# One of the opening input transfers is issued by ScalarE on its own queue instead of by SyncE

## The reference

```python
xn = _gn(x)                          # per sample and group of 16 channels, over H and W
Wc = conv_w[:, :, 0, 4]
def step(prev, x_i):
    y = einsum('oc,nch->noh', Wc, prev) + conv_b[None, :, None]
    y = where(y >= 0, y, prelu_a * y)
    cur = y + x_i
    return (cur, cur)
# forward scan over the 48 columns, then the backward scan over the forward result
out = x + moveaxis(concatenate([bwd_rest, fl[-1:]]), 0, 3)
```

## Time and profile before

| | us |
|---|---|
| median of three runs | 376.42 |
| lowest and highest | 376.38, 376.47 |
| the profiled execution | 376.38 |
| its span in the trace | 374.6 |
| PE busy | 351.7 |
| DVE busy | 286.0 |
| ACT busy | 230.0 |
| POOL busy | 17.3 |

### The profile page before, as it was taken

The page is one execution under the profiler, slowest core; times in us unless marked ns, Lnnn a source line. Parts: engine busy times, 40 slices in busy tenths (PEclk is TensorE's granted clock), DMA queues, the critical chain, the costliest instruction groups (busy, mean ns, idle before and its releaser), DMA issues.

```text
span 374.6 us, 10099 instructions
## 1 busy us (share of the span) xinstructions
PE 351.7 (94%) x3100; PEld 350.6 (94%) x3100; DVE 286.0 (76%) x925; ACT 230.0 (61%) x810; POOL 17.3 (5%) x30
## 2 busy tenths in 40 slices
PE   0279999999999999999999999999999999999996
PEld 0179999999999999999999999999999999999996
DVE  2688899788887887665666878778778787787786
ACT  2886656656556566565565665655656657566564
POOL 2078000000000000000000000000000000000000
PEclk9999999999999999999999999999999999999999
DMA  8998000000000000000000121211212212122122
GB/s 308 429 412 308 2 0 1 0 0 0 1 0 0 1 0 0 0 0 0 0 0 0 59 84 56 84 66 73 84 56 84 82 58 84 61 79 84 56 112 84
DMA packets 10088, 26.30 MB, mean 70 GB/s; under 512 B 1248, under 2 KB 1504, under 8 KB 9440
## 3 DMA queue, kind: packets, MB, share of 16 engines
q1 hardware_dynamic: 10080, 26.22, 18.1%
HBM read 13.63 MB, written 12.58 MB: 70 GB/s over the span
## 4 chain that ended last, share of the span: by engine, by line
PE 91%; DMA 6%; SPq 1%; DVE 1%; ACT 1%; issue 0%; ACTq 0%
PE psum L352 88%; DMA xin<-in_x 6%; PE psum L312 1%; SPq L234 1%; PE psum L302 1%; DVE state L535 0%; DVE state L530 0%; ACT state L382 0%; ACT state L376 0%; PE psum L277 0%; PE psum L273 0%; PE psum L266 0%; ACT above L445 0%; PE psum L295 0%; PE psum L289 0%
## 5 line engine op out<-in xcount | busy, mean ns | idle before, releaser
L352 PE MATMUL psum<-state,w_t 128*128 (+1 forms) x2976 | 332.6, 275 | 0.0
L352 PEld LDWEIGHTS psum<-state,w_t 128*128 128x128 f32 x2976 | 332.5, 192 | 0.0
L445 ACT ACTIVATE above<-psum,params 128x128 f32<-128x128 f32 x376 | 139.7, 372 | 129.6 <-PE psum L352 128.7
L530 DVE TENSOR_TENSOR state<-above,state 128x128 f32 (+1 forms) x376 | 108.4, 288 | 66.1 <-ACT above L445 56.4
L447 ACT ACTIVATE below<-psum,negative 128x128 f32<-128x128 f32 x376 | 139.9, 372 | 0.0
L535 DVE SCALAR_TENSOR_TENSOR state<-below,negative,state 128x128 f32 (+1 forms) x376 | 123.4, 349 | 6.7
L582 DVE TENSOR_TENSOR state<-state,xin (+1 forms) x45 | 30.8, 684 | 0.0
L475 DVE TENSOR_SCALAR state<-xin,mean,rstd 128x320 f32<-128x320 f32 (+2 forms) x72 | 27.9, 435 | 0.0
L457 DVE BATCH_NORM_STATS2 bstat<-xin 128x6 f32<-128x512 f32 x32 | 20.0, 672 | 8.7 <-DMA xin<-in_x 8.7
L266 PE MATMUL psum<-chan,centre 128*128 128x64 f32 (+1 forms) x8 | 2.1, 361 | 18.7 <-DVE chan L471 18.7
L266 PEld LDWEIGHTS psum<-chan,centre 128*128 128x128 f32 x8 | 1.6, 251 | 19.0 <-issue 15.5
(11 more groups left out here) (38 smaller groups left out, 24.6 us busy)
## 6 DMA issues: line engine op xcount, KB each, us to landing
out_y<-state SPq DMA_DIRECT2D x47, 256.0 KB, 2.0
xin<-in_x SPq DMA_DIRECT2D x5, 1536.0 KB, 12.8
xin<-in_x SPq DMA_DIRECT2D x3, 768.0 KB, 21.8
xin<-in_x SPq DMA_DIRECT2D x7, 256.0 KB, 18.1
w_t<-in_w SPq DMA_DIRECT2D x4, 256.0 KB, 10.6
xin<-in_x SPq DMA_DIRECT2D x1, 512.0 KB, 24.1
out_y<-state SPq DMA_DIRECT2D x1, 192.0 KB, 1.9
out_y<-state SPq DMA_DIRECT2D x1, 64.0 KB, 1.6
```

Of the source, the lines that this page charges most:

```text
L352: mm = nc.tensor.matmul(psum[:, 4 * par + o, 0:COLS], w_t[:, k, o * P:(o + 1) * P], xs[k], start=k == 0, stop=k == 3)
L445: nc.scalar.activation(above[:, par, o, :], z, ACT.Relu, bias=params[:, o:o + 1], scale=1.0).then_inc(above_done, 1)
L530: nc.vector.tensor_tensor(sts[o], above[:, par, o, :], sts[o], ALU.add).then_inc(part_done, 1)
```

## The change

The transfer of blocks 2 and 3 leaves SyncE's program and becomes ScalarE's first instruction. Its source, its destination and its semaphore are the same; it goes to ScalarE's own DMA queue. SyncE issues all others in the same order as before, so that its second transfer is now that of blocks 4 and 5.

```diff
--- before.py
+++ after.py
@@ -23,6 +23,8 @@
 PAIRS = {0: 1, 2: 3, 4: 5, 6: 7, 8: 9}
+
+FROM_ACT = 2
 
@@ -227,7 +229,7 @@
         @block.sync
         def _(sp):
-            for b in (b for b in range(NBLK) if b not in PAIRS.values()):
+            for b in (b for b in range(NBLK) if b not in PAIRS.values() and b != FROM_ACT):
                 n1 = (PAIRS[b] if b in PAIRS else b) % N + 1
@@ -361,6 +363,9 @@
         @block.scalar
         def _(act):
+            n0, n1 = FROM_ACT % N, PAIRS[FROM_ACT] % N + 1
+            act.dma_start(xin[:, FROM_ACT // N, n0:n1, :, :], x[FROM_ACT // N, :, n0:n1, :, :]).then_inc(
+                x_loaded[FROM_ACT][0], 16)
             act.wait_ge(counts_set, 6)
```

## The result

The changed kernel takes 380.03 us (median of six runs, 379.93 to 380.18), the kernel before 376.45 us beside it (376.38 to 376.53, six runs). The ratio is 1.0096, 95% interval 1.0086 to 1.0105: slower by 3.58 us. The forecast was 379.8. The profiled execution took 380.03 us at a span of 378.0, against 376.38 and 374.6 before.

The account below looks back on a forecast made before the run. The first transfer's landing at 7.2 us was taken to set, through ScalarE and PE's queue, the start of a fixed-length scan. 376.38 us plus 3.4 us of later landing gave 379.8 us; range 377.0 to 380.4.

Parts of the forecast that it names:

- The scan is a block of fixed length.: Scan's products on PE: no idle time in front of them, so a change in loads moves only their start.
- Two issues moved, worth nothing.: Programs of SyncE (one issue less, 0.42 us) and ScalarE (one more, 0.38 to 0.42 us while idle): no time gained or lost.
- The engines take turns packet by packet.: Opening loads: two queues share by packet, so the first transfer lands 3.4 us later; chance 0.68.
- a lead of one packet: Opening loads: first transfer one packet ahead on each engine finishes one turn earlier, 3.2 us late instead of 3.65.
- The first rival: Opening loads: first transfer keeps its landing near 7.2 us, time 376.4 us; chance 0.15.
- The lag passes to PE in full.: Opening, ScalarE to PE: batch 1's records come 3.4 us later, PE's deviations at 24.9 us, and PE's queue follows.
- "PE, with no idle time to close, sets the end, and both the keep-up products' pace and their number stay.": End of the opening: PE's queue passes the delay on, so the scan starts 3.4 us later (35.35 becomes 38.75).
- The sum.: Whole kernel: 376.38 us of the profiled execution plus 3.4 us gives 379.8 us.
- "These two arrive at the end only some 2.3 us late": End of the opening: ScalarE and VectorE close up their waits and come only some 2.3 us late.
- the low end of 378.5: Whole kernel: both low ends, 3.2 - 1.1 = 2.1 us, with VectorE's 2.3 as the bound if PE's pace came at fixed time.
- block 2 is third in ScalarE's line, not fourth: ScalarE's opening: block 2 was taken as fourth in line, so its earlier landing gains nothing.
- Faster opening.: Loads' start, third rival: second queue fills the engines 0.5 us sooner, first transfer served first, 375.9 us; chance 0.04.

Follow-up runs that it names:

- experiment 9: Changed kernel with ScalarE's issue of blocks 2 and 3 moved behind its wait for the constants, to 1.7 us: 377.41 us, ratio 1.0029.
- the four kernels of this kind: Kernels with two pairs on two queues: the changed one (380.03 us), experiment 1, experiment 7 and the first kernel of experiment 10.
- experiment 2: Changed kernel with only block 3 (768 KB) on ScalarE's queue; SyncE sends blocks 0 and 1, then 2: 377.98 us, ratio 1.0042.
- experiment 3: Changed kernel with ScalarE sending blocks 2 and 3 as two transfers of 768 KB (6 KB packets): 378.15 us, ratio 1.0045.
- experiment 4: Changed kernel with SyncE sending block 0 alone (6 KB packets), then block 1; ScalarE still sends blocks 2 and 3: 377.84 us, ratio 1.0033.
- experiment 6: Kernel before with only the parameters (2.5 KB) moved to the head of ScalarE's program: 376.95 us, ratio 1.0012.
- experiment 1: Changed kernel with queues exchanged: ScalarE issues blocks 0 and 1, SyncE all others: 380.11 us, ratio 1.0098.
- experiment 7: Changed kernel with ScalarE issuing blocks 8 and 9 first instead of 2 and 3: 379.77 us, ratio 1.0090.
- experiment 5: Blocks 2 and 3 on ScalarE's queue as in experiment 3, but cut into eight transfers of 12 columns (1.5 KB packets): 391.44 us, ratio 1.0401.
- experiment 8: Changed kernel with ScalarE waiting for blocks 0 and 1 to land before issuing blocks 2 and 3: 382.68 us, ratio 1.0165.
- first kernel of experiment 10: Changed kernel with the first group of keep-up products cut from 12 in the trace to 4: 379.65 us, ratio 1.0084.
- experiment 11: Kernel before, all on SyncE's queue, with block 0 sent alone ahead of block 1: 376.66 us, ratio 1.0006.

## Why the prediction was right

The direction, the size and the mechanism held; 380.03 us lies in the range of 377.0 to 380.4 and 0.2 us from the forecast. What carries the lag to the end was not what the prediction named, and that the total is so close is partly luck. By its steps:

- **The scan is a block of fixed length.** Shown: 332.6 us of products in both, and VectorE's first state update of the scan goes from 37.90 to 41.30, its last from 372.15 to 375.55, both by 3.40.
- **Two issues moved, worth nothing.** SyncE's and ScalarE's part were right (0.40 us at 0.79, ScalarE idle until 10.95). But experiment 9 shows that the moment of the issue is not free to choose: 0.9 us later is worth 2.6 us (380.03 to 377.41).
- **The engines take turns packet by packet.** The term was 3.4 us (3.2 with a lead of one packet, 3.65 without) and measured 3.74: no lead, the upper end and a little over, 3.50 to 4.05 in the four kernels of this kind. Equal counts in the changed kernel and nearly equal ones in experiments 2, 3, 4 and 6 show the turns; experiments 2, 3 and 4 exclude sharing by bytes. The Trainium skill, page DMA: Bandwidth & Descriptors, section Queues, rings and completion order, says that an engine goes round robin between rows at packet granularity. The trace agrees if a packet is what the profile counts (17 against 17 in a microsecond). If each of these were one of the typical 9 to 17 descriptors that the page gives for a packet, the first transfer's 8 on an engine could have gone in one turn and kept their landing, and it lost 3.74 us.
- **The first rival (landing kept, 376.4 us)** fell in the changed kernel, but it describes experiment 9 in part: there the first queue does finish most of what was queued first. The same page of the Trainium skill says, in its section Issuing engines are not separate DMA queues, that transfers interleave whichever engine starts them, and that several issuing engines only save issue time. The bandwidth bears that out (418 GB/s with two queues). But the interleaving changed what lands first, and that cost 1% of the time; "only saves", taken alone, would have missed it.
- **The lag passes to PE in full.** 3.73 us at the deviations of batch 1, shown.
- **"PE, with no idle time to close, sets the end, and both the keep-up products' pace and their number stay."** Both halves were wrong. The 20 products took 2.96 us, not 3.52, so that PE's side came only 3.2 us late. And POOL sets the end, which the prediction never followed: it starts its last stretch 3.73 us late and has 0.32 us to give, which is 3.40. PE's faster pace gave the scan nothing: in experiment 1 the 20 products took 3.48 us, and VectorE's first state update is 0.33 us less late than the first use of block 0 (3.72 against 4.05), here 0.34 (3.40 against 3.74).
- **The sum.** 3.4 us was the middle between two landings, and the span grew by 3.40 because the landing came 0.34 us later than taken and POOL had 0.32 us of idle time. These two cancel by luck. The rest of the 3.65 us between the profiled executions lies outside the span; some 0.1 of it goes with the second queue (experiment 6), and the prediction had no term for it.
- **"These two arrive at the end only some 2.3 us late"** was wrong. VectorE's last channel record goes from 34.29 to 37.32 us, 3.0 late. I let both engines close their waits for transfers and forgot that ScalarE waits for PE's variances behind the keep-up products (0.91 us at 29.39) and VectorE for ScalarE (0.90 at 30.95). It made no difference to the forecast, as PE was taken to set the end; but the low end of 378.5 rests on it and was too low. (In the same place block 2 is third in ScalarE's line, not fourth, which changes nothing.)
- **Faster opening.** 253 GB/s between 1.75 and 3.50 us with two queues against 281 with one: the second queue doesn't fill the engines sooner.

Open: why the pace of the keep-up products differs. The same 20 took 3.52, 2.96, 3.48, 3.31, 2.77 and 2.53 us (the kernel before, the changed one, experiments 1, 7, 3, 9), at a granted clock of 1.00, or 0.999. It doesn't set the scan's start in those with blocks on the second queue: in the changed kernel and experiments 1 to 5 and 7 to 9, the multiplication that releases the scan stands 10.12 to 10.16 us behind the start of POOL's power of batch 1 (29.73 to 39.87 in the changed one), whatever the pace, and in all but experiment 1 VectorE waits for POOL there. Only the first kernel of experiment 10, where PE's side holds the scan, is apart (10.74 us).

## What to carry to other kernels

When the DMA engines are full, a second queue doesn't add transfers but reorders them: what was to land first now shares with what was to land second, packet against packet, so give everything that the first work waits for the engines to itself, and look at packet sizes, since the queue with the smaller packets loses. Before moving a transfer, list what each landing is waited for by, and how long behind it there is no slack; here one landing at 7.2 us had next to none, and the one moved ahead some 1.7 us (an estimate: landed near 10.87, first used by ScalarE at 12.56). A gain at a point where two limits meet is worth nothing (experiment 11), a loss there is paid nearly in full. And follow every engine that works without a pause up to the end, also one that is busy for 5% of the span: here POOL's line of small operations, not PE's, carried the delay to the scan.

## What the runs showed of the hardware that I had not expected

- **Turns count packets, not bytes.** Against 12 KB packets of the other queue, ScalarE's packets of 12, 6 and 1.5 KB and of some bytes delay the first use of block 0 from 7.21 to 10.95, 9.21, 7.76 and 7.78 us. The last two are nearly alike (0.55 and 0.57 us over 8 turns), but they can't be one fixed cost of a packet: the bytes of eight 1.5 KB packets on each engine account for 0.46 us by themselves (an eighth of 3.65), those of 20 bytes for nothing. A turn of 20 bytes costs about 0.07 us, while the profile gives such a packet only some 0.01 us of its own (1.5% of 16 engines for 29 of them in a microsecond); where the rest goes isn't shown.
- **A queue that starts behind a backlog starts late.** Issued at 0.79 us together with the other queue's first transfer, it moves 24 packets by 4 us; issued at 1.68 it has its first packet between 5.75 and 6 us, issued at 7.07 between 10.75 and 11. That is 4.1 to 4.3 and 3.7 to 3.9 us, a little over the 3.65 that one transfer of eight packets on each engine takes. Whether the transfers already issued stand ahead of it in making the packets or in the engines was not tried.
- **The pace of small products** varies by up to 1 us in 20 of them (2.53 to 3.52) at the same granted clock, as told above.
